# A repetition and a sum change places in TensorE's queue, in a fused scan and attention kernel

## The reference

```
x_dbl = jnp.einsum('bkdl,kcd->bkcl', xs, x_proj_w)
dts, Bs, Cs = jnp.split(x_dbl, [R, R + N], axis=2)
delta = jax.nn.softplus(dts + dt_b[None, :, :, None])
def step(h, inp):
    u_t, dt_t, B_t, C_t = inp
    h = jnp.exp(dt_t[..., None] * A) * h + (dt_t * u_t)[..., None] * B_t[:, :, None, :]
    y = jnp.einsum('bkdn,bkn->bkd', h, C_t)     # the sum over the 16 states
    return (h, y)
```

## Time and profile before

| what | value |
|---|---|
| median of 3 runs | 12685.33 us |
| the profiled execution: its own time, its span | 12669.79 us, 12667.6 us |
| scanning, about 240 to 11925 us of the span | 11685 us |
| VectorE busy in the span | 10108.9 us, 80% |
| GpSimd busy | 9745.3 us, 77% |
| TensorE matmuls busy | 9137.1 us, 72% |
| ScalarE busy | 7125.6 us, 56% |
| mean granted clock of TensorE | 0.717 of full speed |

### The profile page before, as it was taken

How to read it: one execution, slowest core, us unless ns; L and a number is a source line. 1 busy time by engine, 2 the same in 40 slices (tenths; PEclk the granted TensorE clock), 3 DMA queues, 4 the chain that set the end, 5 groups by cost and what they waited for, 6 DMA issues and landing times.

```text
span 12667.6 us, 94576 instructions
## 1 busy us (share of the span) xinstructions
PE 9137.1 (72%) x26432; PEld 2291.2 (18%) x26432; DVE 10108.9 (80%) x5979; ACT 7125.6 (56%) x10802; POOL 9745.3 (77%) x4231
## 2 busy tenths in 40 slices
PE   6866677866778677777767777786777767777665
PEld 2211111211112111211111211121112211122121
DVE  2899987898888988888888887888888888888500
ACT  3655545655556555665556655567456665576424
POOL 1888887888788988888887887887878888888500
PEclk8955576865778567777777877787677867777665
DMA  3666588576765566556665678665775546555310
GB/s 81 144 126 127 126 148 144 127 139 126 151 134 142 121 153 148 136 125 149 146 155 115 139 142 138 136 141 121 143 147 129 144 117 156 141 133 121 96 45 15
DMA packets 1782986, 1636.70 MB, mean 129 GB/s; under 512 B 1323311, under 2 KB 1324625, under 8 KB 1782461
## 3 DMA queue, kind: packets, MB, share of 16 engines
q1 hardware_dynamic: 1782460, 1630.65, 59.1%
HBM read 627.40 MB, written 197.66 MB: 65 GB/s over the span
## 4 chain that ended last, share of the span: by engine, by line
PE 27%; issue 20%; DVE 17%; POOL 16%; ACT 10%; SPq 5%; DMA 4%; DVEq 0%; POOLq 0%; ACTq 0%
POOL pr L1410 10%; DVE hs L1338 8%; DVE ps L1323 7%; PE ps L876 4%; PE ps L694 4%; PE ps L721 4%; PE ps L863 3%; POOL dur L1418 3%; PE ps L854 3%; POOL us L1401 2%; SPq L600 2%; ACT dec L1114 2%; PE ps L838 2%; ACT ps L1114 1%; DVE hs L1334 1%
## 5 line engine op out<-in xcount | busy, mean ns | idle before, releaser
L1410 POOL TENSOR_TENSOR pr<-hs,crep 128x1024 f32<-128x1024 f32 x3072 | 7192.5, 2354 | 1753.2 <-DVE hs L1338 1118.3
L1338 DVE TENSOR_TENSOR_SCAN hs<-dec,carry,ps 128x1024 f32<-128x1024 f32 x1728 | 4053.8, 2346 | 227.9 <-POOL pr L1410 7.7
L1323 DVE TENSOR_TENSOR ps<-ps,dur 128x1024 f32<-128x1024 f32 x2304 | 2791.2, 1211 | 969.6 <-PE ps L863 765.4
L863 PE MATMUL ps<-sbc,selb 96*128 96x512 bf16 x4608 | 1874.6, 503 | 1752.3 <-DVE hs L1338 1187.8
L1114 ACT ACTIVATE dec<-dtr,ac 128x1024 f32<-128x1024 f32 x2304 | 2613.3, 1136 | 423.0 <-DVE hs L1338 415.1
L876 PE MATMUL ps<-pr,red 128*32 128x512 f32 x12288 | 2340.6, 845 | 114.2 <-POOL pr L1410 111.8
L1418 POOL TENSOR_TENSOR dur<-dur,brep 128x1024 f32<-128x1024 f32 x768 | 1808.1, 2354 | 171.9 <-DMA brep<-bc_d 98.4
L1121 ACT ACTIVATE carry<-hs 128x1 f32<-128x1 f32 x2304 | 459.1, 199 | 2543.9 <-DVE hs L1338 2231.1
L1334 DVE TENSOR_TENSOR_SCAN hs<-ps,carry,dur 128x1024 f32<-128x1024 f32 x576 | 1339.4, 2335 | 331.2 <-POOL dur L1418 230.0
L1338 DVE TENSOR_TENSOR_SCAN hs<-dec,zero,ps 128x1024 f32<-128x1024 f32 x576 | 1351.1, 2346 | 72.5 <-DVE ps L1323 2.0
L694 PE MATMUL ps<-xb,tapw 96*96 96x512 f32 x2304 | 1206.1, 638 | 43.4 <-ACT sd L953 40.9
(11 more groups left out here) (117 smaller groups left out, 7088.8 us busy)
## 6 DMA issues: line engine op xcount, KB each, us to landing
dtr<-de SPq DMA_DIRECT2D x768, 512.0 KB, 7.9
dur<-us SPq DMA_DIRECT2D x768, 512.0 KB, 8.5
crep<-bc_d SPq DMA_DIRECT2D x512, 512.0 KB, 6.0
ust<-u_d SPq DMA_DIRECT2D x256, 384.0 KB, 6.1
y_d<-yst SPq DMA_DIRECT2D x768, 128.0 KB, 4.3
sd<-y_d SPq DMA_DIRECT2D x512, 192.0 KB, 4.8
brep<-bc_d SPq DMA_DIRECT2D x128, 512.0 KB, 7.3
u_d<-sd SPq DMA_DIRECT2D x64, 384.0 KB, 3.2
```

The lines of the kernel that those rows point to most:

```text
L863: mm = pe.matmul(ps[:, SLOT + 2 * (n % RS) + hf, :], selb[:, i % GT // 2, :], sbc[:, w % 2, B * hf:B * (hf + 1)], start=True, stop=True)
L1323: dve.tensor_tensor(slot(n), slot(n), dur[:, 2 * (G % 2) + i % 2, :], ALU.mult).then_inc(bu_v, 1)
L1338: dve.tensor_tensor_scan(hs[:, n % RH, :], dec[:, others(n) % RD, :], slot(n), init, ALU.mult, ALU.add).then_inc(scan_v, 1)
L1410: pool.tensor_tensor(pr[:, n % RP, :], hs[:, n % RH, :], crep[:, q, :], ALU.mult).then_inc(prod_g, 1)
```

## The change

In the even turns the pair's sum is issued before the next tile's fill, and no longer behind it. No instruction is added or removed, and the other four engines' queues are the same. Where the next tile has no fill (a group's turns 5 and 6), nothing changes; in turns 0, 2 and 4 of each group the two trade places. That makes nine places in a window and 1150 in the kernel.

```
                 for i in range(NT):
                     n = w * NT + i
+                    if i % 2 == 0 and n >= 4:
+                        reduce2((n - 4) // 2)
                     if n + 1 < W * NT and not on_pool(n + 1):
                         fill(n + 1)
-                    if i % 2 == 0 and n >= 4:
-                        reduce2((n - 4) // 2)
                     for tick in (2 * i, 2 * i + 1):
```

## The result

The changed kernel takes 12705.49 us (median of 20 runs, 12670.15 to 12725.63), the kernel before 12664.69 us (median of 20 runs). The ratio is 1.0029, with a 95% interval of 1.0022 to 1.0035: slower by 0.29%, some 37 us. I had forecast -11 us, no change that can be measured. The time lies in the range that I gave, but the sign was wrong: it is a third of the way to "late fills decide". One thing to keep in mind for the traces: the profiled execution of after took 56 us more than that of before, where the medians differ by 41.

The account below looks back on a forecast made before the run. No engine was taken as full; TensorE, VectorE and GpSimd hand the lead on to each other. 70 - 43 - 38 = -11 us takes 12670 to 12659; with the median 15.5 us higher, 12674, range 12570 to 12800.

Parts of the forecast that it names:

- late fills decide: Rival: in turns 0, 2 and 4 of a group, TensorE late from side work; +120 us, 12805; chance 0.25.
- Term 1: Fills behind a sum in turns 0, 2 and 4 come later and delay VectorE; 0 to 279 us, taken as 70.
- stay in time: Moved fills already in time remain so where TensorE is not behind: a sum's 1.55 or 1.94 us is under 2.43.
- The two covers: A sum waiting for its product (112 us uncovered) or ScalarE's copy (1.7 us) holds up the fill behind; put at nothing.
- my own sign: The forecast is wrong if the sums wait for GpSimd for more than twice 112 us.
- Term 2: Sums come sooner, so GpSimd's 205 waits for them shrink by 0.85 us each; at most 174 us, taken as 43 off.
- Term 3: Sums use TensorE's pause before even turns' fills, so later work starts sooner; at most 115 us, taken as 38 off.
- The clock: Rival: idle time before fills moves, shifting TensorE's mean clock; 0.01 is worth 48 us, 12626 or 12722; chance 0.05.
- The quiet windows: Windows 5 to 14 (687 to 1511 us, 824 us) were to keep their length within 2 us.

## Why the prediction was wrong

**Term 1, the step that failed.** I took a quarter of 279 us, 70, as what late fills leave. The 279 came from spreading the late fills evenly, 180 of 361 in even turns; in truth 65 of them were there, with 162 us. And I counted only fills that were late already, and wrote that fills in time stay in time. After the change 206 of the moved fills are late, with 380 us: 141 that had been in time are not any more, and 218 us of wait came with them. The scans' ends show a loss of 218 us at the same tiles, before what later waits take in. My "stay in time" rested on the 2.43 us that a fill lies ready in rows 8, a place where TensorE is ahead. It left out the many places where TensorE comes late from side work, but by less than that slack; there a sum of 1.06 to 1.94 us uses it up. 213 of the 218 us come from places where TensorE reached the sum from other work without a pause.

**The two covers.** I put the sum's wait for a product at nothing and would call myself wrong above twice 112 us; it is 468. By my own sign that was wrong, but the price was right: VectorE waits 4 us for the fills behind such sums. It is the cover that I had named: the scan of the tile waits for the same product, and sum and fill fit beside it. The wait for the copy went from 1.7 to 144 us, which I had put at nothing as well, and that was right in price too: taking it away changed the time by nothing that can be told.

**Term 2.** GpSimd's wait for sums fell by 190 us, more than the 174 that I gave as the upper end. Its wait for scans rose by 297. How much of it was worth anything, the runs don't show.

**Term 3.** TensorE's idle time before fills fell by 663 us, but 499 of them came back before the sums. Tile 12 gains 75 us, which turn 10 alone gives too (86), and tile 11 pays 51 in front of it. All tiles that were not moved behind a sum gain 164 us, against 81 for terms 2 and 3 together. Those gains were undersized too, by 83, but less than term 1, by 148: 218 - 164 = 54 us in the traces, where I had 70 - 81 = -11. Both are gross sums, since a delay at one tile that a later wait takes in stands in both.

**Rivals.** "Late fills decide" named the right mechanism and place, turns in which TensorE comes late from side work. Its 120 us were too many, since its gains, 20 us, were too low; whether more than one in two late fills was passed on can't be read from these runs. The clock did not move between before and after: 0.714 in both, mean of the runs. It did move within the time, up in the windows in which the norm stands beside turn 10. The quiet windows kept their length, as forecast.

## What to carry to other kernels

When an instruction is moved ahead of another in an engine's queue, ask for each place in the loop whether the engine comes to it early or late; one place that fits does not speak for the rest. Where it comes early and pauses, the moved instruction cost next to nothing here, even where it had to wait for its own operand. Where it comes late, what now stands second is later by the whole length of the first. Counting the places that are late already is not enough: a result that is in time has a slack in us, and one that is in time by less than the moved instruction's length turns late. An order that helps at one turn and hurts at another need not be the same in all turns: here one turn in nine carried the gain, and most of that went with a clock that was higher there.

## What the runs showed of the hardware

Halving three quarters of the sums, which take TensorE 1.06 or 1.94 us each, went with a fall of its mean granted clock from 0.714 to 0.671, and the kernel was 0.26% slower, although the engine had less to do. Between two orders of the same instructions the clock differed by up to 0.007 (0.7105 with turns 4, 12 and 20 ahead, 0.7177 with turns 2, 10 and 18), of which the slower had the lower clock; but the slowest, turns 0, 8 and 16, had 0.7136, so the clock does not set their order. Among runs of one and the same kernel, 0.01 more clock goes with some 44 us less time (standard error 4.5, all kernels pooled). The norm's stretch of 9.5 us in window 33 ran at 0.52 in one order and at 1.00 in the other.
